# Attention and routed experts in one kernel: two sets of transposes go to other PSUM banks, and VectorE's router steps change places

## The reference, cut to what matters

```python
def reference(x, ...):                      # x: 16 x 256 x 256
    h = gelu(other @ W1 + readout @ W2 + b)               # 16 x 255 rows of 256
    # attention, 16 heads of 64 elements, on the normalised rows
    z = layernorm(h)
    q, k, v = split_heads(z @ Wq.T), split_heads(z @ Wk.T), split_heads(z @ Wv.T)
    attn = safe_softmax(q @ k.T * 64 ** -0.5)
    h = h + (attn @ v) @ Wo.T + bo
    # eight experts, the best two of each row, and a shared expert
    xf = layernorm(h)
    probs = softmax(xf @ router_w)
    topw, topi = top_k(probs, 2)
    routed = sum over the two of topw * (silu(xf @ w1[e]) @ w2[e])
    shared = sigmoid(xf @ gate_w) * (silu(gate) * up @ shared_down)
    return h + routed + shared
```

## Time and profile before

| | us |
|---|---|
| median of 3 runs (lowest, highest) | 1081.71 (1078.3, 1083.3) |
| the profiled execution, its own time | 1082.13 |
| the profiled execution, its span | 1080.4 |
| one group in the middle of the main phase | 96 |
| a round with no side work | 9.6 |
| TensorE busy in the span | 1014.5 |

### The profile page before, as it was taken

One profiled execution on the slowest core, in us unless ns is written; L12 is line 12 of the kernel. 1 busy time (PEld: TensorE's weight loads), 2 busy tenths in 40 slices (PEclk: granted clock), 3 DMA queues, 4 the chain that ended last, 5 costly groups with the idle time before them and its releaser, 6 DMA issues.

```text
span 1080.4 us, 23154 instructions
## 1 busy us (share of the span) xinstructions
PE 1014.5 (94%) x8042; PEld 877.6 (81%) x8042; DVE 744.6 (69%) x1912; ACT 661.4 (61%) x1939; POOL 512.6 (47%) x557
## 2 busy tenths in 40 slices
PE   6979999999999999999999999999998899999995
PEld 6867889778887887888787788879786779999985
DVE  3757775776677577767757885775784566666667
ACT  4647774676577477747747784765685445555541
POOL 0016543557356455735554664555435387454430
PEclk9989999999999999999999999999999999999998
DMA  8110000001000000100000010000003643444479
GB/s 272 60 45 2 1 2 1 21 2 40 21 1 22 21 21 1 41 21 1 21 22 21 1 41 21 2 11 31 21 2 127 224 120 110 135 141 130 134 219 312
DMA packets 47496, 65.91 MB, mean 61 GB/s; under 512 B 7992, under 2 KB 39480, under 8 KB 47384
## 3 DMA queue, kind: packets, MB, share of 16 engines
q1 hardware_dynamic: 40056, 44.50, 13.2%
q0 software_dynamic: 7056, 19.93, 5.4%
q10 hardware_dynamic: 272, 0.00, 0.0%
HBM read 36.09 MB, written 28.33 MB: 60 GB/s over the span
## 4 chain that ended last, share of the span: by engine, by line
PE 69%; DVE 10%; ACT 6%; DMA 4%; issue 3%; SPq 2%; POOL 0%; DVEq 0%; ACTq 0%; POOLq 0%
PE proj_ps L70 11%; PE proj_ps L72 11%; PE proj_ps L71 11%; PE proj_ps L738 9%; PE pT_ps L725 9%; PE s_ps L711 8%; DMA back<-expert_out_rows 2%; ACT prob L1041 2%; PE s_ps L70 2%; PE s_ps L71 2%; PE s_ps L72 2%; PE s_ps L963 1%; PE pT_ps L984 1%; DVE probT L1288 1%; DVE z L1389 1%
## 5 line engine op out<-in xcount | busy, mean ns | idle before, releaser
L1041 ACT ACTIVATE prob<-s_ps,nmax 128x255 f32<-128x255 f32 x512 | 238.0, 480 | 154.7 <-DVE nmax L1263 154.6
L1716 POOL TENSOR_SCALAR prob<-prob,rinv 128x255 f32<-128x255 f32 x128 | 138.4, 1081 | 282.3 <-DVE rinv L1281 281.8
L1263 DVE TENSOR_REDUCE nmax<-s_ps 128x2 f32<-128x510 f32 x256 | 157.7, 678 | 7.6 <-PE s_ps L711 7.0
L725 PEld LDWEIGHTS pT_ps<-ident,prob 128*128 128x128 f32 x1024 | 114.6, 140 | 37.1 <-issue 28.5
L725 PE MATMUL pT_ps<-ident,prob 128*128 128x128 f32 x1024 | 137.0, 276 | 3.4 <-ACT probT L1067 3.0
L738 PE MATMUL proj_ps<-probT,v 128*64 128x256 f32 x1024 | 125.7, 387 | 1.5 <-DVE probT L1288 1.3
L1270 DVE TENSOR_TENSOR qk_space<-proj_ps,qk_space 128x512 fp32r<-128x512 f32 x128 | 88.2, 689 | 47.2 <-ACT qk_space L1053 45.2
L1718 POOL TENSOR_SCALAR prob<-prob,rinv 128x255 f32<-128x255 f32 x128 | 119.5, 934 | 0.0
L711 PE MATMUL s_ps<-qk_space 64*128 64x256 f32 x1536 | 109.1, 289 | 0.9 <-DVE qk_space L1270 0.9
L1048 ACT ACTIVATE prob<-prob,rinv 128x255 f32<-128x255 f32 x128 | 66.7, 521 | 70.5 <-DVE rinv L1281 70.4
L1041 ACT ACTIVATION_READ_ACCUMULATOR prob<-s_ps,nmax 128x1 f32 x512 | 108.9, 213 | 0.0
(11 more groups left out here) (257 smaller groups left out, 2701.9 us busy)
## 6 DMA issues: line engine op xcount, KB each, us to landing
xg<-expert_in_rows SPq DMA_DIRECT2D x71, 130.0 KB, 2.2
back<-expert_out_rows SPq DMA_DIRECT2D x6, 1024.0 KB, 21.2
xin<-in_x_dram SPq DMA_DIRECT2D x8, 512.0 KB, 4.9
z_rows<-z SPq DMA_DIRECT2D x8, 512.0 KB, 3.1
z<-z_rows SPq DMA_DIRECT2D x8, 512.0 KB, 4.2
expert_in_rows<-bo_row SPq DMA_DIRECT2D x16, 128.0 KB
raw_up<-in_L_ffn_w_dram SPq DMA_DIRECT2D x8, 256.0 KB, 5.5
raw_down<-in_L_ffn_w_dram SPq DMA_DIRECT2D x8, 256.0 KB, 6.7
```

Source lines behind the costliest of these rows:

```text
L725: m = pe.transpose(pT_ps[h][:, o:o + P], prob[u_par(u)][:, h, qt, kt * P:(kt + 1) * P], ident[:])
L1041: m = act.activation(prob[u_par(u)][:, h, qt, 1:N], s_ps[b][h][:, qt * N + 1:(qt + 1) * N], ACT.Exp, bias=nmax[b][:, n:n + 1], accum_out=r ...
L1263: dve.tensor_reduce(nmax[b][:, 2 * h:2 * h + 2], s_ps[b][h][:].rearrange("p (q k) -> p q k", q=2)[:, :, 1:N], AX_X, ALU.max, negate=True). ...
L1716: pool.tensor_scalar(prob[k][:, 0, 1, 1:N], prob[k][:, 0, 1, 1:N], rinv[k][:, 1:2], None, ALU.mult).then_inc(s_nA1, 1)
```

## The change

- The transposes of z (all groups) and of the router's rows (all but the last group's) are written to `pT_ps[c]` in place of `proj_ps[1 - c]`, and the copies (`z_hi`, `z_lo`, `z2_hi`, `z2_lo`) read from there. Before them TensorE waits for `probT_a` (c=0) and `probT_b` (c=1) of the round's second unit, in place of `qk_lo` and `v_copy`.
- `transpose_p` of unit 4 (first of round p2) and of unit 12 (first of p6) waits for `z2_lo` and `z_lo`, the last readers of the banks. The waits for the same in `values_bank` (p2, p6) and in `next_qk` (p2) go; `values_bank` then waits for `qk_lo` in those rounds as in the plain ones.
- VectorE: `z2_lo` and `z_lo` (two instructions each) go from the end of p1 and p5 to the start of p2 and p6, behind the first of the four maxima. `probabilities` goes from the middle to the end of p3. `row_slots` goes from the middle of p5 to the middle of p6. `layernorm_stats` of two tiles goes from the end of p6 to the middle of p7, of the other two from the end of p7 to the middle of p0 of the next group.
- GpSimd: the first `scatter_rows` of p6 and p7 goes behind the normalising of the second unit.

```diff
--- before.py
+++ after.py
@@ -537,6 +537,10 @@
         FREE_W = 2
 
 
+        def rows_T_ps(c, last):
+
+            return proj_ps[1 - c] if last else pT_ps[c]
+
         def rank_ps(last):
             return z_ps[0] if last else proj_ps[1]
 
@@ -664,12 +668,10 @@
             pe.sem_inc(s_T, FREE_P)
 
             def transpose_z(g, c):
-                ps = proj_ps[1 - c]
+                ps = pT_ps[c]
                 pe.wait_ge(s_z, GT * g + GT)
-                if g and c == 0:
-                    pe.wait_ge(s_qkl, UNITS * g)
-                elif g:
-                    pe.wait_ge(s_ve, ROUNDS * g)
+                if g:
+                    pe.wait_ge((s_pA, s_pB)[c], UNITS * g - 4 + FREE_B)
                 for t in range(GT):
                     m = pe.transpose(ps[:, t * P:(t + 1) * P], z[:, t, c * P:(c + 1) * P], ident[:])
                 m.then_inc(s_zt, 1)
@@ -719,6 +721,10 @@
                     for part in normal:
                         pe.wait_ge(part, u + 1)
                     pe.wait_ge(free, u + FREE_B)
+                    if i == 4 and g:
+                        pe.wait_ge(s_zl2, DC * (g - 1) + h + 1)
+                    elif i == 12 and g + 1 < GROUPS:
+                        pe.wait_ge(s_zl, DC * (g + 1) + h + 1)
                     for kt in range(2):
                         for qt in range(2):
                             o = kt * N + qt * P
@@ -746,14 +752,10 @@
                     return
                 if not first and p == 1:
                     pe.wait_ge(s_woe, 2 * r + 1 + FREE_W)
-                elif not first and p == 2:
-                    pe.wait_ge(s_zl2, DC * r + 1)
                 elif not first and p == 3:
                     pe.wait_ge(s_lr, r + 1)
                 elif not first and p == 5:
                     pe.wait_ge(s_rank_read, r + 1)
-                elif p == 6 and not last:
-                    pe.wait_ge(s_zl, DC * g + DC + 1)
                 elif last and p == ROUNDS - 1:
                     pe.wait_ge(s_ol, ROUNDS * g + p - 1)
                 else:
@@ -778,9 +780,9 @@
                 if c == 0:
                     pe.wait_ge(s_z2, GT * r + GT)
                 if not last:
-                    pe.wait_ge(*((s_qkl, UNITS * (r + 1) + 8), (s_ve, ROUNDS * (r + 1) + 4))[c])
+                    pe.wait_ge((s_pA, s_pB)[c], UNITS * (r + 1) + 4 + FREE_B)
                 for t in range(GT):
-                    m = pe.transpose(proj_ps[1 - c][:, t * P:(t + 1) * P], z2[:, t, c * P:(c + 1) * P], ident[:])
+                    m = pe.transpose(rows_T_ps(c, last)[:, t * P:(t + 1) * P], z2[:, t, c * P:(c + 1) * P], ident[:])
                 m.then_inc(s_zt2, 1)
 
             def router_logits(r, last):
@@ -814,8 +816,6 @@
                 pe.wait_ge(s_ve, ahead)
                 if p == 1 and not first:
                     pe.wait_ge(s_woe, 2 * r + 2 + FREE_W)
-                elif p == 2 and not first:
-                    pe.wait_ge(s_zl2, DC * r + DC)
                 elif p == 6:
                     pe.wait_ge(s_zl, DC * to + DC)
                 project_qk(to, 2 * pair)
@@ -1054,7 +1054,7 @@
 
             def z_hi(g, c):
                 act.wait_ge(s_zt, DC * g + c + 1)
-                act.activation(zT_hi[:, c, :], proj_ps[1 - c][:], ACT.Copy).then_inc(s_zh, 1)
+                act.activation(zT_hi[:, c, :], pT_ps[c][:], ACT.Copy).then_inc(s_zh, 1)
 
             def v_copy(g, p):
                 act.wait_ge(s_v, ROUNDS * g + p + 1)
@@ -1073,7 +1073,7 @@
 
             def z2_hi(r, c):
                 act.wait_ge(s_zt2, DC * r + c + 1)
-                act.activation(z2T_hi[:, c, :], proj_ps[1 - c][:], ACT.Copy).then_inc(s_zh2, 1)
+                act.activation(z2T_hi[:, c, :], rows_T_ps(c, r == GROUPS - 1)[:], ACT.Copy).then_inc(s_zh2, 1)
 
             def router_exps(r):
                 act.wait_ge(s_nm, 2 * r + 2)
@@ -1271,7 +1271,7 @@
 
             def z_lo(g, c):
                 dve.wait_ge(s_zh, DC * g + c + 1)
-                dve.tensor_tensor(zT_lo[:, c, :], proj_ps[1 - c][:], f32(zT_hi[:, c, :]), ALU.subtract).then_inc(s_zl, 1)
+                dve.tensor_tensor(zT_lo[:, c, :], pT_ps[c][:], f32(zT_hi[:, c, :]), ALU.subtract).then_inc(s_zl, 1)
 
             def normalise_a(g, i):
                 u, k = UNITS * g + i, u_par(UNITS * g + i)
@@ -1354,7 +1354,7 @@
 
             def z2_lo(r, c):
                 dve.wait_ge(s_zh2, DC * r + c + 1)
-                dve.tensor_tensor(z2T_lo[:, c, :], proj_ps[1 - c][:], f32(z2T_hi[:, c, :]),
+                dve.tensor_tensor(z2T_lo[:, c, :], rows_T_ps(c, r == GROUPS - 1)[:], f32(z2T_hi[:, c, :]),
                                   ALU.subtract).then_inc(s_zl2, 1)
 
             def router_logits(r):
@@ -1482,6 +1482,12 @@
                     if has_next:
                         for b in range(2):
                             maxima(*nxt, b, 0)
+                            if b == 0 and p == 2 and not first:
+                                z2_lo(r, 0)
+                                z2_lo(r, 1)
+                            elif b == 0 and p == 6 and not last:
+                                z_lo(g + 1, 0)
+                                z_lo(g + 1, 1)
                             maxima(*nxt, b, 1)
                     if p > 0:
                         o_lo(g, p - 1)
@@ -1495,14 +1501,19 @@
                     if not first:
                         if p == 1:
                             normalise_rows(r)
-                        elif p == 3:
-                            probabilities(r)
                         elif p == 4:
                             best_two(r)
                             one_hot(r)
                         elif p == 5:
                             places(r)
+                        elif p == 6:
                             row_slots(r)
+                    if p == ROUNDS - 1 and g + 2 < GROUPS:
+                        layernorm_stats(g + 2, 0)
+                        layernorm_stats(g + 2, 1)
+                    elif p == 0 and not first and g + 1 < GROUPS:
+                        layernorm_stats(g + 1, 2)
+                        layernorm_stats(g + 1, 3)
                     if has_tile:
                         qk_lo(to, 2 * pair + 1)
                     if last and p == ROUNDS - 1:
@@ -1516,19 +1527,12 @@
                             row_stats(r, 0)
                             add_rows(r, 1)
                             row_stats(r, 1)
-                        elif p == 1:
-                            z2_lo(r, 0)
-                            z2_lo(r, 1)
                         elif p == 2:
                             router_logits(r)
+                        elif p == 3:
+                            probabilities(r)
                         elif p == 4:
                             read_ranks(r, False)
-                    if p == 5 and not last:
-                        z_lo(g + 1, 0)
-                        z_lo(g + 1, 1)
-                    if p >= ROUNDS - 2 and g + 2 < GROUPS:
-                        for t in (2 * (p - ROUNDS + 2), 2 * (p - ROUNDS + 2) + 1):
-                            layernorm_stats(g + 2, t)
                 if last:
                     split_shared_lo()
                     o_lo(g, ROUNDS - 1)
@@ -1749,13 +1753,12 @@
                         row_rstd(g - 1)
                     if has_next:
                         normalise_b(nxt[0], 2 * nxt[1])
-                    if not first and p >= ROUNDS - 2:
-                        scatter_rows(g - 1, 2 * (p - ROUNDS + 2))
                     if has_next:
                         normalise_b(nxt[0], 2 * nxt[1] + 1)
                     if not first and p == 2:
                         mark_rows(g - 1)
                     elif not first and p >= ROUNDS - 2:
+                        scatter_rows(g - 1, 2 * (p - ROUNDS + 2))
                         scatter_rows(g - 1, 2 * (p - ROUNDS + 2) + 1)
                     if p == 0 and not last:
                         layernorm_rstd(g + 1)
```

## The result

The changed kernel takes **1056.8 us** (median of 4 runs, 1054.91 to 1058.51); beside it the kernel before took 1080.72 us (4 runs, 1078.3 to 1083.3: the three of the first table and one more). The ratio is 0.9775, with a 95% interval of 0.9755 to 0.9794: 23.9 us less, where 21.0 were forecast. The profiled execution took 1057.78 us, with a span of 1056.0.

The account below looks back on a forecast made before the run. The prediction took TensorE's own list to bound the groups, the change aiming at its gaps. 8.75 (p1) + 13.8 and 0.9 (p5) - 2.4 (p2, p6) = 21.0 us off 1081.7 gave 1060.7 us, range 1053.5 to 1069.

Parts of the forecast that it names:

- What bounds the kernel: In the groups: the path is TensorE's own list, with 21.8 us idle before the transposes of z and router's rows.
- The rival that the prediction weighed there: By weight-load share, the plain round is at 84%; low parts' 1.2 us paid in full 14 times, gain 6.6 us.
- p1: Router's rows: c=1 waits for `probT_b`, scores 1.25 us earlier, 8.75 us in seven groups; some 0.5 us of wait stays.
- p5: Transposes of z: no wait worth counting, scores 2.3 us earlier, 13.8 us in six groups; first group about 0.9 us.
- p2 and p6: Low parts behind the first maximum delay `o_lo` and the k tile: 0.17 us charged 14 times, 2.4 us.
- The second rival: In p2 and p6 the chain through `o_lo` costs 0.6 to 1.2 us per round: 1066 to 1075 us; chance 13%.
- All idle goes: Rival: `o_lo` in time in p2 and p6, c=1 in p1 without a wait; 27 us gained, 1055 us; chance 10%.
- The waits change their name only: Rival: c=1 waits for `probT_b` as long as it did for `v_copy`; 1080 us; chance 4%.
- The slower rival: `z_hi` queues on ScalarE, VectorE stands at `z_lo` with three maxima behind it; 7 us slower, 1089 us; chance 4%.
- The moved steps: `row_slots` in p6, `layernorm_stats` in p7 and p0, `probabilities` at p3's end, and the scatters: all counted at nothing.
- The last group: `row_slots` leaves its p5 too, but its tail waits on ScalarE: counted 0, at most 0.6 us.
- The sum: Whole kernel: 8.75 + 13.8 + 0.9 - 2.4 = 21.0 us off 1081.7, giving 1060.7 us.

Follow-up runs that it names:

- p1_swap: Changed kernel with `probT_b` of the second unit ahead of `qk_lo` of k in round p1 alone; 1053.13 us.
- lo_second: Changed kernel with the low parts (`z2_lo`, `z_lo`) behind the second of the four maxima of p2 and p6 in place of the first; 1055.8 us.
- rows_back: Changed kernel with the router's rows' transposes alone back on `proj_ps`, `z2_lo` back at the end of p1, z staying on `pT_ps`; 1066.0 us.
- late_lo: Changed kernel with the low parts (`z2_lo`, `z_lo`) behind all four maxima of p2 and p6 in place of the first; 1067.85 us.
- moves_only: Changed kernel with both sets of transposes back on `proj_ps` with their old waits, `z_lo` and `z2_lo` back in p5 and p1; other moves stay; 1074.09 us.
- banks_only: Changed kernel with `row_slots`, `probabilities`, `layernorm_stats` and the scatters back in their old places, transposes staying on `pT_ps`; 1062.5 us.
- best: Changed kernel with low parts behind the second maximum, `probT_b` ahead of `qk_lo` in p1 and `probabilities` in the middle of p3; 1051.75 us.
- prob_mid: Changed kernel with `probabilities` back in the middle of p3; 1056.34 us in one run.

## Why the prediction was right, point by point

**What bounds the kernel: right.** The groups go by TensorE's own list. Wherever an experiment took idle time from TensorE the group became shorter by it (p1_swap, lo_second), and where one brought it back it became longer by it (rows_back, late_lo). The rival that the prediction weighed there would have made it 6.6 us; the gain was paid nearly in full, in p5 with matmuls at 10.47 of 10.47 us and weight loads at 8.80. The Trainium skill (Perfetto Trace Analysis, Identifying the Most-Contended Engine) would judge TensorE's headroom by the work done against the peak and by the share of the weight loads, and not by that of the matmuls; in these rounds the share of the matmuls was the one that told.

**p1: right in mechanism, 0.07 us per group too small.** 1.25 was forecast, 1.32 measured (9.28 in seven groups). The step that was off is the hand-over. `probT_b` ends 10.30 us after p1's scores in both kernels (281.06 + 0.68 - 271.44 below; 286.39 - 276.08 in the earlier trace rows), and the count gave TensorE 0.1 more before it starts; it started 0.05 behind it, at 281.79. The 0.15 of the one pair of rows that the prediction took was no constant. The wait that was to stay, some 0.5 us, is 0.22 in the list and 0.44 from start to start (p1_swap). VectorE in p1 and p2 after the change:

```profile
280.46 0.68 DVE L1270 TENSOR_TENSOR qk_space<-proj_ps,qk_space 128x512 fp32r<-128x512 f32 x1
281.06 0.68 DVE L1288 COPY probT<-pT_ps 128x512 f32<-128x512 f32 x1
...
283.39 0.69 DVE L1263 TENSOR_REDUCE nmax<-s_ps 128x2 f32<-128x510 f32 x1 [0.97 <-PE s_ps L713]
283.99 1.27 DVE L1357 TENSOR_TENSOR z2T_lo<-pT_ps,z2T_hi 128x512 fp32r<-128x512 f32 x2
285.19 1.87 DVE L1263 TENSOR_REDUCE nmax<-s_ps 128x2 f32<-128x510 f32 x3
287.44 0.69 DVE L1293 TENSOR_TENSOR oT_lo<-proj_ps,oT_hi 128x512 fp32r<-128x512 f32 x1 [0.38 <-ACT oT_hi L1072]
```

**p5: right.** 2.3 us per group was forecast, 2.31 measured in six groups (13.87 us), and 0.89 in the first group against 0.9. That no wait would be left is seen in the run of eight above, and that it needs both halves of the change in moves_only (11.74) and banks_only (11.47).

**p2 and p6: right in the chain, 0.07 us per round too large.** 0.17 was charged, 0.10 measured: 1.4 us in 14 rounds where 2.4 stood. The chain is the one that the prediction followed. In the rows above the first maximum starts 1.01 us after the scores (1.02 counted), and `o_lo` 5.06 after them (5.16 counted), done at 288.13. On TensorE the k tile of that round, the weight load (PEld) that opens it, and the same tile in lo_second, where nothing waits:

```profile
288.20 0.48 PE L70 MATMUL proj_ps<-zT_hi,wk_lo 128*128 128x512 f32 x1
288.52 0.39 PE L71 MATMUL proj_ps<-zT_lo,wk_hi 128*128 128x512 f32 x1
...
288.18 0.19 PEld L70 LDWEIGHTS proj_ps<-zT_hi,wk_lo 128*128 128x128 f32 x1 [0.25 <-DVE oT_lo L1293]
...
288.75 0.39 PE L70 MATMUL proj_ps<-zT_hi,wk_lo 128*128 128x512 f32 x1
288.97 0.39 PE L71 MATMUL proj_ps<-zT_lo,wk_hi 128*128 128x512 f32 x1
...
288.52 0.19 PEld L70 LDWEIGHTS proj_ps<-zT_hi,wk_lo 128*128 128x128 f32 x1
```

From L70 to L71 it is 0.32 us here and 0.22 in lo_second: the tile is 0.09 late. What waits is the weight load, once in each of the 14 rounds:

```profile
PEld proj_ps L70 <- DVE oT_lo L1293: 3.5, 14, 0.3
```

It starts 0.05 behind `o_lo` and 5.80 us after the scores; in lo_second it starts 5.61 after them (288.52 - 282.91). So it is 0.20 late, of which 0.09 comes out at the matmuls. The prediction set an `o_lo` at TensorE at 6.0 against the start of the matmul at 5.82; both were too late by about 0.2, so that the small size came out near is in part luck. That this is the chain, and not the new wait of `transpose_p`, is shown by lo_second, which moved only the low parts behind one more maximum and lost the 0.10. The second rival, the same chain at 0.6 to 1.2 us per round, is out by size. Its mechanism was there at a tenth of a microsecond.

**All idle goes: closer in time than the forecast, not in mechanism.** That rival stood at 1055, and 1056.8 is nearer to it than to 1060.7. But it wanted no wait at c=1 and an `o_lo` in time, and both waits are there, at 0.22 and 0.09 us. best, where both are gone, has p1 at 10.50 us: 1.76 less than before, which is that rival's own count. *The waits change their name only* is out: `probT_b` is waited for, for 0.22 us and not for 1.2.

**The slower rival: out.** `z2_lo` (L1357 above) starts at 283.99, 0.60 behind the maximum before it as the maxima follow one another, with no idle time: the copies of ScalarE were in time. late_lo shows what a late low part does, 11 us over the run; the mechanism is real, only its cover held.

**The moved steps: right but for one.** `row_slots` in p6, `layernorm_stats` and the scatters cost nothing (banks_only). `probabilities` did: the step of the prediction that failed is "`probabilities` at the end of p3 makes the first maximum of p4 some 0.4 late, less than the slack before `qk_hi`". It was right on the lateness: p4's maxima start 1.40 us after the scores, where they started at 1.02, and VectorE's `qk_lo` of q starts 6.65 us after them in both kernels, so the slack takes it all. What it left out is GpSimd, whose step for the first unit comes 0.38 us later in the round and there meets a small instruction of VectorE (last section). p4 sums to 77.72 us in place of 77.14. It is 0.6 us of 24.

**The last group.** Counted at 0, at most 0.6: its p5 fell from 10.22 to 9.59 us, and the tail gave back part of it. The gain at the last group's p6 scores is 24.72 us (810.15 to 785.43), of the two profiled executions 24.35.

**The sum.** Saved by the medians: 23.9 us against 21.0, 2.9 more. Of that p1 is 0.5, the charge for `o_lo` 1.0, p4 -0.6 and the last group 0.6, together 1.5 us. For the other 1.4 there is a candidate, a term that the prediction didn't have, seen in the profiled execution of before on which its sum stood: in the seventh group's p6 the scores and the values ran slower, once (the usual rows are 1.70 and 1.95 us):

```profile
715.25 2.56 PE L711 MATMUL s_ps<-qk_space 64*128 64x256 f32 x24
717.75 2.62 PE L738 MATMUL proj_ps<-probT,v 128*64 128x256 f32 x16
```

and the windows of these two rows, with the end of the p5 ahead of them and the same stretch one group earlier (columns as above, the granted clock third from the end):

```profile
613.10:619.35 6.25, 4.31 (x32) 3.60 (x30) 4.59 (x19) 3.85 (x11) 3.02 (x4) 1.00 0.00 0
709.00:715.25 6.25, 4.32 (x32) 3.60 (x30) 4.59 (x19) 3.85 (x11) 3.03 (x4) 1.00 0.00 0
715.25:717.75 2.50, 2.50 (x26) 2.27 (x25) 2.27 (x4) 0.97 (x3) 1.77 (x3) 0.60 0.02 7
717.75:720.30 2.55, 2.55 (x19) 1.37 (x17) 1.38 (x3) 1.55 (x8) 0.00 (x0) 0.73 0.00 0
```

The granted clock fell to 0.50, the lower level of 1.2 GHz, for some 3.4 us from 715.7 on, and this p6 lasted 11.15 us in place of 9.60: 1.55 us. Ahead of it TensorE had stood idle for 0.66 and 1.28 us, the very pauses that the change removes. They don't always cost that: the p5 of the group before was the same to 0.01 us, and the clock stayed at 1.00. The Trainium skill (TensorE: Matmul & The Clock Gate, Part 1) says that the window in which TensorE's activity is watched runs freely and isn't reset when a kernel starts. That would let one and the same pause fall on either side; the two stretches agree with it, and no run here tests it. No other kernel's trace has such a fall in the rounds that the table counts. The prediction's rows are all at 1.00, and so it left this out; with it the terms make about 24 us, the medians 23.9. That the runs without a profile have such falls is not shown. Their mean granted clock is on record: 0.988 to 0.991 in the 16 runs of the kernel before that stand beside the experiments, 0.990 to 0.994 in the four of the changed kernel, and a fall of 3.4 us to 0.50 takes 0.0016 off the mean (1.7 of 1080 us). Where in those runs the clock fell isn't recorded, and moves_only, which keeps most of the pauses, is at 0.989 to 0.994: the cause of this 1.4 us, as of the 3.1 us that banks_only has beyond its rounds, stays open. The rest of the distance to 1060.7 is that a fourth run, of 1079.74 us, took the median of the kernel before from 1081.7, where the forecast started, to 1080.7.

## What to carry to other kernels

When one engine's own list is the bound and its idle time stands before a few lines, read for each of these lines what each of its semaphores would release by itself, sorted by time: the gain of taking one away is the distance to the next, and that next one (here `probT_b`, then `row_slots` in front of it) is the next edit. On the engine that releases it, put that step first, and what only feeds the next round behind it. A step moved into a slack must be followed to every engine that it makes late, and losses of 0.1 us per round are seen in the lengths of the rounds where a median can't show them.

## What the runs showed of the hardware

**A small cast held beside GpSimd.** In p4 VectorE converts the experts' indices (L1325, `top_f`), 32 elements per partition. After the change, on VectorE and GpSimd:

```profile
304.76 2.48 DVE L1263 TENSOR_REDUCE nmax<-s_ps 128x2 f32<-128x510 f32 x4
...
311.30 0.43 DVE L1325 CAST top_f<-top_at 128x32 f32<-128x32 uint32 x1
...
312.13 0.68 DVE L1270 TENSOR_TENSOR qk_space<-proj_ps,qk_space 128x512 fp32r<-128x512 f32 x1
...
310.76 0.93 POOL L1722 TENSOR_SCALAR prob<-prob,rinv 128x255 f32<-128x255 f32 x1
```

The cast takes 0.43 us and ends at 311.73, 0.04 behind the end of GpSimd's normalising step (310.76 + 0.93 = 311.69). Before the change, in the same round:

```profile
317.16 0.18 DVE L1325 CAST top_f<-top_at 128x32 f32<-128x32 uint32 x1
...
316.24 0.94 POOL L1718 TENSOR_SCALAR prob<-prob,rinv 128x255 f32<-128x255 f32 x1
```

There it started as GpSimd's step ended (317.18) and took 0.18. Worked out from both engines' timelines, in us from the start of p4's scores (the groups 2, 3, 4, 6, 7 and 8 are alike within 0.03; the fifth has GpSimd later):

| kernel, groups | GpSimd's step (L1718, L1722) | cast starts, takes | `qk_lo` of k starts | p4 |
|---|---|---|---|---|
| before, six groups | 7.02 to 7.96 | 7.94, 0.18 | 8.52 | 9.65 |
| before, the fifth | 7.29 to 8.22 | 7.93, 0.33 | 8.66 | 9.65 |
| prob_mid, six groups | 7.02 to 7.95 | 7.94, 0.18 | 8.52 | 9.64 to 9.66 |
| prob_mid, the fifth | 7.29 to 8.22 | 7.94, 0.32 | 8.66 | 9.66 |
| after, six groups | 7.40 to 8.33 | 7.94, 0.43 | 8.76 | 9.71 to 9.81 |
| after, the fifth | 7.67 to 8.60 | 8.07, 0.18 | 8.65 | 9.67 |

The cast starts at the same place in all three kernels, but for 0.13 us in the last row. What moved is GpSimd's step, 0.38 us later since p4's maxima and the softmax inverses are; where it still runs, the cast ends 0.04 us behind it. With `qk_lo` of k at 8.66 p4 is as before, at 8.76 it isn't: of the 0.25 us for which the cast is held a tenth or so comes out at TensorE. There the ranks must wait for that `qk_lo` (they use its bank). After the change they start 9.59 us after the scores, 0.14 behind its end at 312.13 + 0.68; before it they started 9.51 after them:

```profile
312.95 0.18 PE L807 MATMUL proj_ps<-taken,before 128*128 128x32 bf16 x1
...
318.73 0.19 PE L805 MATMUL proj_ps<-taken,before 128*128 128x32 bf16 x1
```

In two groups, this one among them, the scores behind the ranks lose another 0.07 to 0.08 us, which is not explained. The eight casts after the change (count; shortest, median and longest in ns; the last, behind the loop, has no GpSimd step beside it):

```profile
L1325 DVE CAST top_f<-top_at x8: 180/422/428, 218.8 to 831.2; 128x32 f32<-128x32 uint32 x8
```

The Trainium skill (SBUF — State Buffer, SBUF: two separate sides) says that VectorE and GpSimd share one pair of ports as an exclusive lock: a VectorE step in a two-port mode, or one with two inputs in SBUF beside a GpSimd step that reads SBUF, and the GpSimd step exclude each other, whoever starts first holding the pair for the whole instruction. It counts casts among the steps that can be in such a mode. Six of the seven casts in the loop after the change agree, and the fifth group's before it. The fifth group's after it doesn't:

```profile
496.57 0.18 DVE L1325 CAST top_f<-top_at 128x32 f32<-128x32 uint32 x1
496.78 0.23 DVE L1329 TENSOR_TENSOR hot<-iota,top_f 128x64 f32<-128x64 f32 x1
...
496.17 0.93 POOL L1722 TENSOR_SCALAR prob<-prob,rinv 128x255 f32<-128x255 f32 x1
```

Here the cast and the comparison behind it, which has two inputs, ran at their usual speed inside GpSimd's step. This cast began 0.40 us into the step; the held ones began 0.54 (after) and 0.64 us (before, the fifth group) into theirs. Other small steps with one input, after the change, fall the same way: in p6 of six groups the cast L1350 and the step L1351 began 0.41 and 0.48 us into such a step of GpSimd and took their usual 0.16; in p7 of two groups the step L1279 began 0.65 and 0.68 into one, took 0.31 and 0.27 in place of 0.16, and ended 0.03 behind it. What decides stays open; no run was made on it, and GpSimd's spans are rough.

**The clock in the tail.** Behind the groups every trace has stretches at the lower clock, one or more of 3 to 10 us, at other places in each: 848.9 to 852.3 us before the change, 860.2 to 863.6 after it. The longest is that of rows_back, 834.6 to 844.9 us, and its profiled execution is the slowest of that kernel's four runs (1068.3). The changed kernel's four runs had a mean granted clock of 0.994 at 1054.91 and 1055.81 us, 0.993 at 1057.78 and 0.990 at 1058.51. Such stretches are a likely source of the scatter of some 2 us between runs of one kernel, which is why the small terms were read from the rounds.
